# Four norms applied on ScalarE, experts chosen for four images at a time, queries and keys split from a held PSUM buffer

## The reference, cut to what matters

```python
def _layernorm(x, axis=-1, eps=1e-05):
    m = jnp.mean(x, axis=axis, keepdims=True)
    v = jnp.var(x, axis=axis, keepdims=True)
    return (x - m) / jnp.sqrt(v + eps)

h = _layernorm(x) * (1 + ca) + sa                     # "first" norm of a layer
x = x + ga * attention(h)                             # layer 1: attention norms h again ("inner")
h = _layernorm(x) * (1 + cb) + sb                     # "second" norm
x = x + gb * experts(h)                               # layer 1: rows first times rsqrt(mean(h*h) + 1e-6)

# in attention, for every head
scores = einsum('bhqd,bhkd->bhqk', q, k) / sqrt(Hd) + bias
out = einsum('bhqk,bhkd->bhqd', softmax(scores), v)

# in experts of layer 0
g = softmax(h @ Wr); top2_w, top2_idx = top_k(g, 2); top2_w = top2_w / sum(top2_w)
out = sum(top2_w * (relu(h @ W1[e]) @ W2[e]) for e in top2_idx)
```

## Time and profile before

| | us |
|---|---|
| median of 3 runs | 2116.31 (2114.59 to 2121.39) |
| the profiled execution | 2124.9, its span 2123.1 |
| busy: PE, DVE, ACT, POOL | 1614.7, 1540.6, 1002.2, 878.5 |
| setup | 0 to 61 |
| attention, layer 0 | 61 to 814 |
| experts, layer 0 | 814 to 1108.7 |
| attention, layer 1 | 1108.7 to 1917 |
| experts, layer 1 | 1917 to 2123 |

### The profile page before, as it was taken

The page is one execution under the profiler, slowest core; times in us unless marked ns, Lnnn a source line. Parts: engine busy times, 40 slices in busy tenths (PEclk is TensorE's granted clock), DMA queues, the critical chain, the costliest instruction groups (busy, mean ns, idle before and its releaser), DMA issues. The chain is left out here.

```text
span 2123.1 us, 43990 instructions
## 1 busy us (share of the span) xinstructions
PE 1614.7 (76%) x14050; PEld 1145.8 (54%) x14050; DVE 1540.6 (73%) x4940; ACT 1002.2 (47%) x1846; POOL 878.5 (41%) x932
## 2 busy tenths in 40 slices
PE   2388888888888863999981777777777777753996
PEld 1256555555656542999971444444444444433886
DVE  4378878888888743777753879889888988853664
ACT  0166566666665541222221455565565565541543
POOL 0123353544444432555552335454445454430544
PEclk9899999999999986999995899999999999986998
DMA  4333343343333313222226544554455554525543
GB/s 112 75 67 65 78 74 79 75 79 74 79 74 77 68 39 77 72 72 74 72 58 165 96 87 103 113 110 105 110 110 103 114 111 104 98 63 163 134 124 82
DMA packets 267468, 193.11 MB, mean 91 GB/s; under 512 B 26095, under 2 KB 257297, under 8 KB 266468
## 3 DMA queue, kind: packets, MB, share of 16 engines
q1 hardware_dynamic: 251880, 155.28, 34.7%
q0 software_dynamic: 15360, 35.03, 5.4%
HBM read 95.21 MB, written 53.18 MB: 70 GB/s over the span
## 5 line engine op out<-in xcount | busy, mean ns | idle before, releaser
L871 DVE TENSOR_REDUCE mx<-A 128x2 f32<-128x512 f32 x1024 | 685.6, 681 | 196.2 <-PE A L1131 170.3
L725 ACT ACTIVATE probs<-B 128x1024 f32<-128x1024 f32 x512 | 523.2, 1022 | 370.1 <-PE B L1151 188.8
L1131 PE MATMUL A<-stack 126*128 126x256 bf16 x2048 | 393.5, 281 | 139.5 <-DVE mx L871 110.9
L1151 PE MATMUL B<-stack 128*128 128x256 bf16 x2048 | 360.2, 278 | 64.6 <-DMA stack<-mrow 64.6
L1131 PEld LDWEIGHTS A<-stack 126*128 126x128 bf16 x2048 | 163.0, 99 | 302.3 <-DVE mx L871 205.6
L1169 PE MATMUL M<-probs,vals 128*32 128x256 f32 x4096 | 287.2, 397 | 27.5 <-DVE On L894 24.7
L1151 PEld LDWEIGHTS B<-stack 128*128 128x128 bf16 x2048 | 196.8, 101 | 122.4 <-DMA stack<-mrow 87.5
L626 POOL TENSOR_TENSOR h<-xn,back_rows 128x256 f32<-128x256 f32 x64 | 46.3, 724 | 496.6 <-DVE xn L826 496.6
L640 POOL DMA_INDIRECT gathered<-h,slot_in x192 | 187.1, 974 | 100.7 <-DVE slot_in L1017 52.1
L1580 PE MATMUL A<-w2s,hid 128*128 128x128 f32 x1792 | 219.6, 276 | 8.4 <-issue 8.4
L1580 PEld LDWEIGHTS A<-w2s,hid 128*128 128x128 f32 x1792 | 208.8, 192 | 12.8 <-issue 12.8
(11 more groups left out here) (181 smaller groups left out, 2510.9 us busy)
## 6 DMA issues: line engine op xcount, KB each, us to landing
stack<-parts SPq DMA_DIRECT2D x768, 64.0 KB
xt<-gathered SPq DMA_DIRECT2D x112, 132.0 KB, 2.2
probs<-gathered SPq DMA_DIRECT2D x40, 256.0 KB, 3.2
w<-in_w SPq DMA_DIRECT2D x4, 2048.0 KB, 10.0
back_rows<-mod_rows SPq DMA_DIRECT2D x64, 128.0 KB, 3.7
x_mid<-X SPq DMA_DIRECT2D x64, 128.0 KB, 2.4
hid<-expert_out SPq DMA_DIRECT2D x64, 128.0 KB
X<-in_x SPq DMA_DIRECT2D x32, 128.0 KB, 3.7
```

Source lines behind the costliest of these rows:

```text
L725: act.activation(probs[c % 4][:, :, :, :], Bp[c % 2][:, :, :, :], ACT.Exp, scale=EXP_SCALE[l][c // 4]).then_inc(b_exp.handle, 1)
L871: dve.tensor_reduce(mx[u][:, h, :], A[h % 2][:, :, :], AX.X, ALU.max).then_inc(a_max.handle, 1)
L1131: ins = pe.matmul(A[h % 2][:, t, :], stack[u][0:n, h, 0, t * P:(t + 1) * P], stack[u][0:n, h, 1, :], start=True, stop=True)
L1151: ins = pe.matmul(Bp[c % 2][:, j, t, :], stack[u][:, h, 1, t * P:(t + 1) * P], stack[u][:, h, 0, :], start=True, stop=(l == 1))
```

## The change

1. **Norms.** `first_norm` and `second_norm` of both layers move from DVE to ACT: two instructions of 128x128 with scale = reciprocal root and bias = shift, one column each. DVE computes the shift, -mean times the reciprocal root, in one operation on 128x2 (`first_shift`, `second_shift`). `rms_norm` moves to ACT with a scale column alone. `inner_norm` stays on DVE.
2. **Choosing.** `GROUP` is 4, `HELD` 8, `LAG` 7; the choosing runs once for four images with operations twice as wide, and `scatter` stands at -7. To make room, the experts' weights and `hid` share the memory of h3, and `Y` that of `yt`.
3. **Queries and keys.** `project_qk` writes B0 instead of M0, after chunk 0's exponential. Chunks 1, 2 and 3 all use B1, and chunk 4 waits for the split to have read B0. ACT writes the high part from PSUM, DVE the remainder, ACT the middle part, POOL the low part. The scale of the queries is multiplied into `wq` in the setup. Fewer steps wait for M0.

```diff
-GROUP = 2
+GROUP = 4
-HELD = 4
+HELD = 8
+OUT = 4
-LEAD, LAG = 3, 5
+LEAD, LAG = 3, 7
+BUFFER = (0, 1, 1, 1, 0, 1, 0, 1)
+HOLD = 4
 # POOL
-                ch.link(pool.tensor_tensor(p[:, :, 0, :], qk[:, :, :], one, ALU.mult))
-                ch.link(pool.tensor_tensor(rem[:, :, :], qk[:, :, :], p[:, :, 0, :], ALU.subtract))
-                ch.link(pool.tensor_tensor(p[:, :, 1, :], rem[:, :, :], one, ALU.mult))
-                pool.tensor_tensor(p[:, :, 2, :], rem[:, :, :], p[:, :, 1, :], ALU.subtract).then_inc(split.handle, 1)
+            def low_part(b, k, u):
+                pool.wait_ge(qk_mid.handle, qk_mid.after(b))
+                pool.tensor_tensor(parts[u][:, :, 2, :], rem[:, :, :], parts[u][:, :, 1, :], ALU.subtract)\
+                    .then_inc(split.handle, 1)
-                if at(-5):
-                    scatter(*held(at, -5))
+                if at(-7):
+                    scatter(*held(at, -7))
 # ACT
+            def normed(x, scale, dst, sig, bias=None):
+                for t in range(NT):
+                    if bias is None:
+                        ins = act.activation(dst[:, t, :], x[:, t, :], ACT.Copy, scale=scale[:, t:t + 1])
+                    else:
+                        ins = act.activation(dst[:, t, :], x[:, t, :], ACT.Identity, bias=bias[:, t:t + 1],
+                                             scale=scale[:, t:t + 1])
...
-            def read_qk(b, k, u):
+            def high_part(b, k, u):
                 act.wait_ge(qk_proj.handle, qk_proj.after(b))
...
+                src, dst = Bp[0][:, 0, :, :], parts[u][:, :, 0, :]
                 if l:
+                    ins = act.activation(dst, src, ACT.Copy)
                 else:
+                    ch.mark(act.activation(dst[:, 0, :], src[:, 0, :], ACT.Identity, bias=qs_bias[:, 0:1]))
+                    ins = act.activation(dst[:, 1, :], src[:, 1, :], ACT.Identity, bias=qk_bias[:, 1:2])
+            def mid_part(b, k, u):
+                act.wait_ge(qk_rem.handle, qk_rem.after(b))
+                act.activation(parts[u][:, :, 1, :], rem[:, :, :], ACT.Copy).then_inc(qk_mid.handle, 1)
...
-                step(read_qk, 1)
+                step(high_part, 1)
                 chunk(2)
+                layer(0, first_norm, 2)
                 layer(1, first_rsqrt, 2)
                 step(max_rows, -1, 1)
+                step(mid_part, 1)
                 chunk(3)
                 step(values, 0)
+                layer(1, first_norm, 2)
                 layer(1, second_rsqrt, -2)
                 layer(0, read_on, -2)
                 chunk(4)
+                if l and at(-2):
+                    second_norm(*held(at, -2))
...
                 chunk(6)
+                if l == 0 and at(-2):
+                    second_norm(*held(at, -2))
                 layer(1, inner_rsqrt, 2)
                 layer(1, rms_rsqrt_of, -2)
+                if l and at(-2):
+                    rms_norm(*held(at, -2))
                 step(max_rows, 0, 0)
                 chunk(7)
 # DVE
+            def shift_of(mv, rs, dst, sig):
+                dve.scalar_tensor_tensor(out=dst[:, :], in0=mv[:, :, 0], scalar=-1.0, in1=rs[:, :], op0=ALU.mult,
+                                         op1=ALU.mult).then_inc(sig.handle, 1)
+            def remainder(b, k, u):
+                dve.wait_ge(qk_high.handle, qk_high.after(b))
+                dve.wait_ge(split.handle, split.after(b - 1))
+                src, high = Bp[0][:, 0, :, :], parts[u][:, :, 0, :]
+                if l:
+                    ins = dve.tensor_tensor(rem[:, :, :], src, high, ALU.subtract)
...
                 maxima(6, 1)
+                step(remainder, 1)
                 group(0, choose_first, -3)
                 rows(1, second_stats, -2)
-                layer(1, outer_norm, 2)
                 maxima(7, 1)
+                layer(1, first_shift, 2)
                 step(split_max, 0, 0)
                 maxima(8, 1)
-                layer(1, modulate_rows, 2)
                 layer(1, gated_base, 0)
                 maxima(9, 1)
+                layer(1, second_shift, -2)
+                layer(1, modulate_rows, 2)
...
-                rows(1, second_norm, -2)
-                rows(0, second_norm, -2)
-                rows(1, rms_norm, -2)
 # PE
             def project_qk(b, k, u):
                 pe.wait_ge(h_ready.handle, h_ready.after(b))
-                pe.matmul(M0[:, 0:S], wq[:, l, :], hT[u][:, :], start=True, stop=True)
+                pe.wait_ge(qk_rem.handle, qk_rem.after(b - 1))
+                pe.wait_ge(b_exp.handle, b_exp.after(b - 2, 1))
+                pe.matmul(Bp[0][:, 0, 0, :], wq[:, l, :], hT[u][:, :], start=True, stop=True)
...
                 if at(-3):
-                    m0_read((qk_f32, 1))
                     gate(*at(-3))
```

More of the change, by code:

```diff
@@ L214, in build @@
         rs2 = sb("rs2", [P, NT])
+        shift = [sb(f"shift{u}", [P, NT]) for u in range(2)]
+        shift2 = sb("shift2", [P, NT])
         xn2 = sb("xn2", [P, NT, D])
@@ L1053, in tick @@
                 maxima(2, 2)
-                layer(0, first_norm, 2)
+                layer(0, first_shift, 2)
                 layer(1, added_stats, 2)
@@ L1140, in turn_max, with scores_b @@
                 ins.then_inc(m_T.handle, 1)
-            def scores_b(b, k, u, c):
+            def scores_b(b, k, u, c, hold):
                 if c % 4 == 0:
                     pe.wait_ge(m_in[u][c // 4], m_in.of(k))
-                pe.wait_ge(b_exp.handle, b_exp.after(b, c - 1) if c >= 2 else b_exp.after(b - 1, HH + c - 1))
+                if c == HOLD:
+                    if hold is None:
+                        pe.wait_ge(b_exp.handle, b_exp.after(b, 1))
+                    else:
+                        pe.wait_ge(qk_rem.handle, qk_rem.after(hold))
+                else:
+                    last = [d for d in range(c) if BUFFER[d] == BUFFER[c]]
+                    pe.wait_ge(b_exp.handle, b_exp.after(b, last[-1] + 1) if last else b_exp.after(b - 1, HH + c - 1))
                 for j in range(2):
@@ L1230, in tick @@
                     m0_read((h_ready, 1), (mT_read, -1, 1), (mT_read, -2, 2))
+                    if not at(-1) and group_done(at, -5):
+                        pe.wait_ge(pos_read.handle, pos_read.after(at(-5)[1]))
                     turn_h2(*held(at, -3))
@@ L1312, in experts @@
     xt_in = Transfers([sem(f"xt_in{u}") for u in range(2)], 1)
-    yt_out = Transfers([sem(f"yt_out{v}") for v in range(HELD)], NT, 0)
+    yt_out = Transfers([sem(f"yt_out{v}") for v in range(OUT)], NT, 0)
     extra_in = Transfers([sem(f"extra_in{u}") for u in range(2)], 1)
@@ L1389, in _ @@
                     scatter(*tile(k, n))
-            for s in range(slots - HELD, slots):
-                pool.wait_ge(yt_out[s % HELD], yt_out.of(s // HELD))
+            for s in range(slots - OUT, slots):
+                pool.wait_ge(yt_out[s % OUT], yt_out.of(s // OUT))
         @block.vector
@@ L1627, in inputs_of @@
         rows[part, :, :, 1] = k_side[:, None, :]
+    q_scale = np.stack([np.where(np.arange(D) < 64, HD ** -0.5, (2.0 / HD) ** 0.5), np.full(D, D ** -0.5)], 1).astype(np.float32)
     max_rows = np.zeros((2, H, 2, S))
@@ L1652, in inputs_of @@
         "qk_bias": np.stack([bqkv[0:D][stacked], bqkv[D:2 * D][stacked]], 1),
-        "q_scale": np.stack([np.where(np.arange(D) < 64, HD ** -0.5, (2.0 / HD) ** 0.5), np.full(D, D ** -0.5)], 1).astype(f),
+        "q_scale": q_scale, "scale_row": np.broadcast_to(q_scale.T[None], (P, 2, P)).copy(),
         "vo_bias": np.stack([bqkv[2 * D:][out_rows], n["L0_attn_b_out"]], 1),
```

170 lines of the change are left out of this document (86 added, 84 removed).

## The result

The changed kernel takes 2144.78 us in the median (2141.49 to 2147.19), the kernel before 2117.79 in the same runs; the ratio is 1.0125 with an interval of 1.0108 to 1.0141. It is slower, where 24 us less were forecast.

The account below looks back on a forecast made before the run. No engine was full; a loop of maxima, split, transposition, copy and DMA of `mrow`, and chunk 0 closed each tick. Ticks -10 and -28, leads -3, tails +10 and +5, setup +2 gave -24: 2092 us, range 2046 to 2144.

Parts of the forecast that it names:

- Prices: Estimated operation times: norm pair on ACT 0.80 us, `rms_norm` pair 0.65, middle part 0.59, DVE's remainder 0.68, shift 0.17.
- The lock: Layer 1: DVE's add of L917 falls from 1.222 us to 0.43 (-0.80) with three split operations fewer on POOL.
- Layer 0: Layer 0's 31 ticks: four ticks take 84.7 us instead of 85.96, -10 us in all.
- Layer 1, up to the copy of `mrow`: Layer 1's ticks: four take 86.3 us instead of 89.98, -3.7, or -28 in all, from less DVE work and halved choosing.
- and 2.42 to chunk 0: Layer 1's tick sum: from the copy of `mrow` to chunk 0 pass 2.42 us, within a tick of 21.0 without choosing.
- The second rival: PE is held at chunk 0 whenever DVE is early; halved choosing's -14 is eaten by fixed +14: 2116 us, chance 0.14.
- Its sign: At chunk 0, PE's wait for the `mrow` DMA growing beyond 1 us a tick would show the second rival.
- Tails and leads: Outside the ticks: layer 0's tail +10 us, layer 1's tail +5, leads about -1.5 a layer, -3 in all.

Follow-up runs that it names:

- the split alone: The kernel before with only the queries-and-keys part of the change (held buffer, split over ACT, DVE, ACT, POOL): 2098.7 us, ratio 0.9903 to the kernel before.
- the norms alone: The kernel before with only the norms part of the change (norms applied on ACT, shifts on DVE): 2129.5 us, ratio 1.0045 to the kernel before.
- the group alone: The kernel before with only the choosing part of the change (four images at a time, scatter two ticks later): 2144.4 us, ratio 1.0107 to the kernel before.
- rms_late: The changed kernel with `rms_norm` behind the copy of `mrow` on ACT instead of ahead of it: 2150.8 us, ratio 1.0113 to the kernel before.

## Why the prediction was wrong

By its own steps:

- **Prices.** Near. The norm on ACT was taken as 0.43 and took 0.482 (each 128x128 with two columns), its pair as 0.80 and took 83.7 / 96 = 0.87, `rms_norm`'s pair as 0.65 and took 0.69, the middle part 0.59 and 0.62, the remainder 0.68 and 0.68, the shift 0.17 and 0.15 in the median, but 0.30 in the mean. The Trainium skill's figures ("ScalarE: Activation LUTs", "What ACT_TABLE_LOAD costs") give an estimate of 0.479 for one such norm and 0.87 for the pair, better than my middle.

```profile
L693 ACT ACTIVATE xn<-X,shift,rs 128x128 f32<-128x128 f32 x192 | 83.7, 484 | 5.3 <-DVE shift L877 2.5
L691 ACT ACTIVATE shared<-h,rs 128x128 f32<-128x128 f32 x64 | 22.2, 393 | 1.1
L734 ACT ACTIVATE parts<-rem 128x512 bf16<-128x512 f32 x64 | 39.8, 622 | 24.2 <-DVE rem L913 21.7 <-DVE rem L917 2.5
L913 DVE TENSOR_TENSOR rem<-B,parts 128x512 f32<-128x512 f32 x32 | 21.8, 682 | 0.6 <-DVE mv L851 0.6
```

- **The lock.** Right. The add of L917, now L971, is 0.426 us in all 32 places. It is so with the split alone too, while the norms alone and the group alone leave it at 1.11 and 1.13 in the mean:

```profile
L971 DVE TENSOR_TENSOR shared<-On,xb x32: 425/426/427, 1201.8 to 1905.7; 128x256 f32<-128x256 f32 x32
```

- **Layer 0.** Right in sign, -14.3 for -10, but by other parts. Of the -10 some -6 were the group's; alone it gave -3, the split -12, the norms +6.
- **Layer 1, up to the copy of `mrow`.** Right: -3.7 forecast, -3.7 measured per four ticks, but between the q,k copy and the copy of `mrow` only.
- **Layer 1, the step that failed:** "and 2.42 to chunk 0". I took the time from the copy of `mrow` to chunk 0 as a constant, from two ticks in which SP's transfers ahead were through. It is 2.4 to 6.2 us, in the mean of ticks 6 to 29 3.45 (2.65 before), and it grew when the copy came earlier into the same traffic, as rms_late shows. The kernel before had two such ticks among layer 1's (3.76 and 5.95 us), which I did not weigh. With it went a second constant, PE's pace: 3.82 us from chunk 0 to the q,k copy at a clock of 1.00, up to 6.6 at 0.54, mostly behind a long wait. Together +6.6 us per four ticks.
- **The second rival** (the DMA's wait takes the place of DVE's time) named the right mechanism, but priced it as no gain. What it lacked is that the wait overshoots, and that PE is slower behind it. Its sign, a wait beyond 1 us a tick, told nothing: the 0.53 of the earlier trace rows was a low one, and PE's wait at chunk 0 was 1.05 us in the mean before and 2.12 after. The growing ticks of 21.06, 22.11, 25.95 and 29.68 fit a chain of late chunk 0, late split, late loads and more traffic at the next copy.
- **Tails and leads.** Layer 0's tail was sized at +10 and measured +7.5 (the last scatter starts 57.2 us behind the last maximum instead of 49.7). The leads, sized at -1.5 each, gave nothing back that the stretches show (+2.2 for +0.5 up to the first maximum). Layer 1's tail was sized at +5 and measured +10: four DMAs more (5.1 us), and the last slot numbers are 5.3 us later behind the last maximum (35.1 instead of 29.8). That is 33.8 with the norms alone and 31.8 with the group alone, so both parts add to it.

```profile
1902.18 0.17 DVE L1017 CAST slot_in<-r 128x4 int32<-128x4 f32 x1
```
```profile
1918.88 0.17 DVE L1058 CAST slot_in<-r 128x8 int32<-128x8 f32 x1
...
1928.74 0.96 POOL L642 DMA_INDIRECT gathered<-shared,slot_in  x1 [0.30 <-issue]
```

Shown by experiment: the group of four is the part that loses most, and layer 1's norms on ACT lose too; the scatters' place accounts for 14 us of layer 1; PE's standing still lowers its clock and costs 1.1%; ACT's order of `rms_norm` costs nothing; an earlier copy of `mrow` is answered by a longer way to chunk 0. Moving the loads gave 0.8%. Argued from the traces only: that loads and stack transfers make up the rest of the wait, and the chain by which one late tick makes the next later.
